# Fewer and larger transfers for the row-tile stacks and the maxima, values copied early, and the maxima split on GpSimd, in a float32 attention and FFN block

## What is computed

```python
x = x + attention(LN(x))      # 16 heads of 16: xw = x_h @ w_att_val[h]; softmax(xw @ x_h^T / 4) @ vx; out projection
x = x + ffn(LN(x))            # gate, up, down (704 wide); inputs, weights and h in blockwise FP4, silu(gate) * up
```

## Time and profile before

| | |
|---|---|
| median of 3 runs | 1744.99 us |
| the profiled execution, its own time | 1744.46 us |
| its span, first to last instruction | 1742.7 us |
| first block | 0 to about 55 us |
| stacks of batch 0, first max scores | 55 to 89 us |
| 16 batches of attention | 89 to about 1165 us |
| FFN | to 1742.7 us |
| PE busy over the span | 88% |
| DVE busy over the span | 77% |
| ACT, POOL busy over the span | 50%, 35% |

### The profile page before, as it was taken

One profiled execution on the slowest core, in us unless ns is written; L12 is line 12 of the kernel. 1 busy time (PEld: TensorE's weight loads), 2 busy tenths in 40 slices (PEclk: granted clock), 3 DMA queues, 4 the chain that ended last, 5 costly groups with the idle time before them and its releaser, 6 DMA issues. The chain is left out here.

```text
span 1742.7 us, 34245 instructions
## 1 busy us (share of the span) xinstructions
PE 1525.8 (88%) x8874; PEld 928.7 (53%) x8874; DVE 1343.5 (77%) x2731; ACT 866.4 (50%) x1778; POOL 605.2 (35%) x740
## 2 busy tenths in 40 slices
PE   3388888888898888888888989878999999999998
PEld 3144445455444454454454444445666666666666
DVE  7577676676686776766766857728999999999995
ACT  2056565565665655655656647653333333333332
POOL 2124324333333343243333332213334433333332
PEclk8589999998998998998999989998999999999999
DMA  4523343333343333333343333300000000000000
GB/s 153 147 75 106 105 111 98 101 100 106 93 111 92 107 100 99 110 98 105 100 102 98 110 89 97 113 2 3 19 15 15 15 15 15 15 15 15 15 18 18
DMA packets 82531, 127.34 MB, mean 73 GB/s; under 512 B 28864, under 2 KB 48448, under 8 KB 82368
## 3 DMA queue, kind: packets, MB, share of 16 engines
q1 hardware_dynamic: 74720, 119.55, 23.9%
q10 hardware_dynamic: 7776, 7.36, 1.4%
HBM read 81.67 MB, written 45.15 MB: 73 GB/s over the span
## 5 line engine op out<-in xcount | busy, mean ns | idle before, releaser
L1071 DVE TENSOR_REDUCE neg_max<-ring 128x1 f32<-128x512 f32 x1024 | 649.8, 679 | 212.8 <-PE ring L865 210.9
L1002 ACT ACTIVATE probs<-scores 128x512 f32<-128x512 f32 x1024 | 528.6, 604 | 273.5 <-PE scores L876 273.4
L865 PE MATMUL ring<-x_stack,q_stack 64*128 64x512 f32 x1024 | 247.3, 480 | 127.3 <-DVE o_rows L1123 49.4
L1408 PE MATMUL gu_bank<-splits,f_x_T 128*128 128x352 f32 x1024 | 317.4, 464 | 2.1 <-ACT f_x_T L1386 2.1
L892 PE MATMUL ring<-probs,v_quad 128*32 128x512 f32 x2048 | 279.6, 668 | 1.6 <-DVE o_rows L1123 0.8
L865 PEld LDWEIGHTS ring<-x_stack,q_stack 64*128 64x128 f32 x1024 | 103.3, 197 | 299.9 <-DVE neg_max L1071 152.6
L873 PE MATMUL scores<-q_stack,x_stack 64*128 64x512 f32 x1024 | 216.2, 417 | 36.4 <-DMA max_stack<-max_rows 35.9
L1408 PEld LDWEIGHTS gu_bank<-splits,f_x_T 128*128 128x128 f32 x1024 | 191.6, 192 | 99.3 <-issue 3.0
L723 POOL TENSOR_TENSOR pv_rows<-pv_more,pv_rows 128x512 f32<-128x512 f32 x64 | 82.2, 1284 | 422.3 <-ACT pv_more L1008 420.9
L876 PE MATMUL scores<-max_stack,max_ones 64*128 64x512 f32 x1024 | 211.4, 407 | 0.0
L1236 POOL TENSOR_TENSOR f_rstd<-f_mean_var,eps 128x1 f32<-128x1 f32 x64 | 44.7, 699 | 330.7 <-DVE f_mean_var L1346 330.7
(11 more groups left out here) (130 smaller groups left out, 2102.3 us busy)
## 6 DMA issues: line engine op xcount, KB each, us to landing
q_stack<-q_split SPq DMA_DIRECT2D x512, 64.0 KB, 2.4
x_stack<-x_split SPq DMA_DIRECT2D x256, 128.0 KB, 2.7
x_split<-splits SPq DMA_DIRECT2D x64, 256.0 KB, 2.2
q_split<-splits SPq DMA_DIRECT2D x64, 256.0 KB, 2.3
out_dram<-x_all SPq DMA_DIRECT2D x64, 128.0 KB, 1.7
x_all<-in_L_attn_x_dram ACTq DMA_DIRECT2D x14, 512.0 KB, 5.5
max_rows<-max_turned SPq DMA_DIRECT2D x256, 4.0 KB, 1.8
max_stack<-max_rows SPq DMA_DIRECT2D x128, 8.0 KB
```

Source lines behind the costliest of these rows:

```text
L865: pe.matmul(bank(tiles[m])[:, :], row_tile(q_stack[q], m)[:, p, s * P:(s + 1) * P], row_tile(x_stack[q], m)[:, p, :], start=True, stop=Tru ...
L1002: act.activation(probs[j][:, k, :], scores[k][:, :], ACT.Exp).then_inc(p_ready, 1)
L1071: dve.tensor_reduce(neg_max[g % 2][:, at:at + 1], tile[:, :], AX.X, ALU.max, negate=True).then_inc(m_used, 1)
L1408: m = pe.matmul(gu_bank[c][:, :], x_T[u][:, a, :], gate_up_T[:, a, c * CH:(c + 1) * CH], start=(a == 0), stop=(a == HALVES - 1))
```

## The change

The stacks are loaded with one transfer per row tile and tensor: 4 for a quad instead of 12. For this the stored keys are written four times, in the order of the row tile (xh, xl, xl, xh; the order of the pieces changes, and each key piece still meets the same query pieces: hh, lh, ll and hl in another order), and the query pieces are read twice by a source pattern with a leading dimension of two copies. The stored queries stay qh, ql; a q row tile is now qh, ql, qh, ql. The turned maxima go to DRAM with one transfer instead of four. GpSimd does the two splitting instructions of the maxima, DVE only the turn, one place later in the step. The copies of the values move to earlier steps of GpSimd's order. STORES counts six transfers of a half on one semaphore.

```diff
+STORES = (4 + 2) * 16
-    x_split = dram("x_split", [B, HALVES, 2, D, HH, T], F32)
-    q_split = dram("q_split", [B, HALVES, 2, D, HH, T], F32)
+    x_rows = dram("x_rows", [B, HALVES, 4, D, HH, T], F32)
+    q_rows = dram("q_rows", [B, HALVES, 2, D, HH, T], F32)
...
-                store(a, x_split, xh, xl, x_stored)
+                store(a, x_rows, (xh, xl, xl, xh))
...
-    POOL_STEP = {(0, 0): ("values",), (0, 1): ("halves", "x0"), (0, 3): ("q0",),
-                 (1, 0): ("values",), (1, 1): ("halves",),
-                 (2, 0): ("values",), (2, 1): ("halves", "x1"), (2, 2): ("deviation",), (2, 3): ("q1",),
-                 (3, 0): ("normal0", "values"), (3, 1): ("halves", "normal1"), (3, 2): ("normal2",),
+    POOL_STEP = {(0, 0): ("maxima", "values0"), (0, 1): ("halves", "x0", "values1"), (0, 3): ("q0", "values2"),
+                 (1, 0): ("maxima", "values3"), (1, 1): ("halves",),
+                 (2, 0): ("maxima",), (2, 1): ("halves", "x1"), (2, 2): ("deviation",), (2, 3): ("q1",),
+                 (3, 0): ("maxima", "normal0"), (3, 1): ("halves", "normal1"), (3, 2): ("normal2",),
                  (3, 3): ("normal3",)}
...
+            def split_maxima(i, g, start):
+                u, n = g % 2, QUAD * TT
+                pool.wait_ge(m_used, n * (i + 1))
+                if not start:
+                    pool.wait_ge(m_turned, i - 1)
+                pool.tensor_tensor(max_cols[u][:, 0:n].bitcast(F32R), neg_max[u][:, :],
+                                   one[:, :].broadcast_to([P, n]), ALU.mult).then_inc(m_split, 1)
+                pool.wait_ge(m_split, i + 1)
+                pool.tensor_tensor(max_cols[u][:, n:2 * n].bitcast(F32R), neg_max[u][:, :],
+                                   max_cols[u][:, 0:n], ALU.subtract).then_inc(m_low, 1)
...
                 for m in range(ROWS):
                     h = h0 + PAIRS * m
-                    for k in range(4):
-                        src = q_split[bass.ds(b, 1), a, k // 2, :, h:h + PAIRS, :]
-                        sp.dma_start(row_tile(q_stack[g], m)[D * k:D * k + D, :, :].bitcast(F32),
-                                     src.rearrange("o d h t -> (o d) h t")).then_inc(stack_loaded[g], 16)
-                    for k in range(2):
-                        src = x_split[bass.ds(b, 1), a, :, :, h:h + PAIRS, :]
-                        sp.dma_start(row_tile(x_stack[g], m)[2 * D * k:2 * D * k + 2 * D, :, :].bitcast(F32),
-                                     src.rearrange("o l d h t -> (o l d) h t")).then_inc(stack_loaded[g], 16)
+                    src = x_rows[bass.ds(b, 1), a, :, :, h:h + PAIRS, :]
+                    sp.dma_start(row_tile(x_stack[g], m).bitcast(F32),
+                                 src.rearrange("o k d h t -> (o k d) h t")).then_inc(stack_loaded[g], 16)
+                    src = q_rows[bass.ds(b, 1), a, :, :, h:h + PAIRS, :].rearrange("o k d h t -> (o k d) (h t)")
+                    sp.dma_start(row_tile(q_stack[g], m).bitcast(F32),
+                                 src.unsqueeze(0).broadcast_to([2, 2 * D, PAIRS * T])).then_inc(stack_loaded[g], 16)
...
                 sp.wait_ge(m_turned, i + 1)
-                for r in range(TT):
-                    sp.dma_start(max_rows[bass.ds(i, 1), :, r, :].rearrange("o c t -> (o c) t"),
-                                 max_turned[g % 2][32 * r:32 * r + 32, :]).then_inc(max_stored, 16)
-                sp.wait_ge(max_stored, 16 * TT * (i + 1))
+                sp.dma_start(max_rows[bass.ds(i, 1)].rearrange("o c r t -> (o r) c t"), max_turned[g % 2][:, :])\
+                  .then_inc(max_stored, 16)
+                sp.wait_ge(max_stored, 16 * (i + 1))
...
-            def max_part(part, i, g, start):
...
+            def turn_maxima(i, g, start):
+                dve.wait_ge(m_low, i + 1)
+                if not start:
+                    dve.wait_ge(max_stored, 16 * (i - 1))
+                dve.transpose(max_turned[g % 2][:, :], max_cols[g % 2][:, :]).then_inc(m_turned, 1)
...
-                        if j == 0 and s < 3 and turning:
-                            max_part(s, i + 1, (g + 1) % QUADS, first and g == 0)
+                        if j == 0 and s == 3 and turning:
+                            turn_maxima(i + 1, (g + 1) % QUADS, first and g == 0)
```

More of the change, by code:

```diff
@@ L112, in build @@
                 minus_half=minus_half, eps=eps, ident=ident, x_all=x_all, out_T=out_T, out_bias=out_bias,
-                x_split=x_split, q_split=q_split, gate_up_kept=gate_up_kept, down_kept=down_kept, sems=sems,
+                x_rows=x_rows, q_rows=q_rows, gate_up_kept=gate_up_kept, down_kept=down_kept, sems=sems,
             )
@@ L173, in first_block @@
                           "qh_done"))
-    x_stored, q_stored = ([sems[f"{n}_stored{a}"] for a in range(HALVES)] for n in "xq")
+    stored = [sems[f"stored{a}"] for a in range(HALVES)]
     x_first, gu_loaded, dn_loaded, vw_loaded, ow_loaded, qw_loaded, bias_loaded, kept = (
@@ L223, in load_x, with store @@
                              x[at:at + n].rearrange("b (s p) e -> p (b s) e", p=P)).then_inc(loaded, 16)
-            def store(a, dst, high, low, stored):
-                for k, t in enumerate((high, low)):
+            def store(a, dst, rows):
+                for k, t in enumerate(rows):
                     sp.dma_start(dst[0:1, a, k].rearrange("o d h t -> (o d h) t"), t[:, a, :].bitcast(F32))\
@@ L257, in _ @@
             for a in range(HALVES):
-                sp.wait_ge(x_stored[a], 32)
-                sp.wait_ge(q_stored[a], 32)
+                sp.wait_ge(stored[a], STORES)
             sp.wait_ge(kept, 16 * (len(GU_CHUNKS) + 2))
@@ L538, in attention_block @@
                           "qh_done"))
-    x_stored, q_stored = ([sems[f"{n}_stored{a}"] for a in range(HALVES)] for n in "xq")
+    stored = [sems[f"stored{a}"] for a in range(HALVES)]
     x_loaded, ffn_loaded = sem("x_loaded"), sem("ffn_loaded")
-    STACK = ROWS * 6 * 16
+    STACK = ROWS * 2 * 16
     pool_set, v_spread = sem("pool_set"), sem("v_spread")
@@ L754, in batch @@
                 first = isinstance(b, int) and b == 0
+                last = isinstance(b, int) and b == B - 1
                 for g in range(QUADS):
@@ L757, in batch @@
                         for task in POOL_STEP.get((g, j), ()):
-                            if task == "values":
-                                ready_values(b, g, first)
+                            if task == "maxima":
+                                if not (last and g == 3):
+                                    split_maxima(QUADS * b + g + 1, (g + 1) % QUADS, first and g == 0)
+                            elif task[:6] == "values":
+                                ready_values(b, int(task[6]), first)
                             elif task == "halves":
@@ L772, in _ @@
             pool.wait_ge(pool_set, set_up())
+            split_maxima(0, 0, True)
             batch(0)
@@ L783, in load_stacks, with store @@
                 a, h0 = g * QUAD // HH, g * QUAD % HH
-                sp.wait_ge(x_stored[a], 32 * (b + 1))
-                sp.wait_ge(q_stored[a], 32 * (b + 1))
+                sp.wait_ge(stored[a], STORES * (b + 1))
                 for m in range(ROWS):
                     h = h0 + PAIRS * m
-                    for k in range(4):
-                        src = q_split[bass.ds(b, 1), a, k // 2, :, h:h + PAIRS, :]
-                        sp.dma_start(row_tile(q_stack[g], m)[D * k:D * k + D, :, :].bitcast(F32),
-                                     src.rearrange("o d h t -> (o d) h t")).then_inc(stack_loaded[g], 16)
-                    for k in range(2):
-                        src = x_split[bass.ds(b, 1), a, :, :, h:h + PAIRS, :]
-                        sp.dma_start(row_tile(x_stack[g], m)[2 * D * k:2 * D * k + 2 * D, :, :].bitcast(F32),
-                                     src.rearrange("o l d h t -> (o l d) h t")).then_inc(stack_loaded[g], 16)
-            def store(c, a, dst, name, high, low, stored):
+                    src = x_rows[bass.ds(b, 1), a, :, :, h:h + PAIRS, :]
[4 more added lines that the diff above has]
+                                 src.unsqueeze(0).broadcast_to([2, 2 * D, PAIRS * T])).then_inc(stack_loaded[g], 16)
+            def store(c, a, dst, name, rows):
                 sp.wait_ge(x_low if name[0] == "x" else q_low, HALVES * (c - 1) + a + 1)
-                for k, t in enumerate((high, low)):
+                for k, t in enumerate(rows):
                     sp.dma_start(dst[bass.ds(c, 1), a, k].rearrange("o d h t -> (o d h) t"),
@@ L1171, in _ @@
                 if g == 0:
-                    for part in range(3):
-                        max_part(part, g, g, True)
+                    turn_maxima(g, g, True)
             batch(0)
```

35 lines of the change are left out of this document (10 added, 25 removed).

## The result

The changed kernel takes 2004.16 us (four runs, 1997.34 to 2015.10) against 1745.17 us for the kernel before, run beside it: ratio 1.149, 95% interval 1.143 to 1.155. It is 259 us slower. The forecast was 1927 us with a range of 1850 to 2120.

What follows compares the result with a forecast made beforehand. Bound taken: PE's stalls in the attention loop and the slow clock after them. Batch 78.8 us, 10.5 over 68.3, times 15 is 158; plus 24.5 before batch 0, sum 182 on 1744.46, giving 1927 us; range 1850 to 2120.

Steps and rivals of the forecast that it cites:

- The engines of a transfer: SyncE's transfers: q loads, whose pattern begins with 2, use 2 engines, 72 packets each per stack, 12.7 us.
- Cost of a packet: Stack loads on two engines: 0.176 us per 4 KB packet, ends 0.15 and 0.235; a stack lands after 14.9 us.
- 0.14 us: Packet time by the skill page's 27 GiB/s per engine; the sum would be some 80 us above today.
- The waits: PE waits for stacks or maxima at quad starts: 9.7 us at quad 2, none at 3, 5.7 at 0, 1.5 at 1.
- 3.8 + 17.6 = 21.4 against 15.7: Quad 0: q1 stored 3.8 us behind quad 2's end, maxima 17.6 later, quad 3 lasting 15.7; wait 5.7 us.
- The clock: PE's slow clock after a stall over 2 us: 2.0 us each behind the waits at quads 2 and 0.
- 57.9: Batch in us without the stalls: quads of 57.2 plus 0.7 for POOL being late in quad 1.
- Values early: Fourth values copy on POOL moves from (3, 0) to (1, 0), removing quad 3's stall: 5.8 us a batch gained.
- A: Quad 3's start: PE stalls 3.38 us behind DVE's v_dense and POOL's last values copy; 5.8 us a batch with slow clock.
- The maxima store: One SyncE issue for four saves 1.4 us per quad; its 128 B pieces stay as many.
- All 16 engines: Rival: all 16 engines serve the q loads, quad 2's stall also goes, batch 10.4 us less; 1586 us, chance 0.10.
- The rate of short transfers (2200 us): Rival: two engines at 0.235 us a packet, a stack 16.9 us, batch 96 us; 2200 us, chance 0.10.

Runs made afterwards that it cites:

- two q transfers: Changed kernel with each q_stack row tile loaded by two transfers of 32 rows instead of one beginning with 2; 1619.41 us, ratio 0.927 to the kernel before.
- the copies inside: Changed kernel, still one q load per row tile, but its source is 32 rows by 2 copies and q pieces are stored to match; 1646.88 us, ratio 0.943.
- The last two versions: Two q transfers with POOL's maxima first and even quads' maxima stored before stack loads, 1582.54 us; then also x tiles loaded before q is stored, 1571.17 us.
- the transfers alone: Changed kernel with the GpSimd part undone: new transfers, values and maxima as in the kernel before; 1980.50 us, ratio 1.135.

## Why the prediction was right

The direction, the cause and the range held; the time was 77 us too low. The packets of SyncE's queue on the page of the kernel before, for the first point:

```profile
q1 hardware_dynamic: 74720, 119.55, 23.9%
```

- **The engines of a transfer.** Read from the completions in the earlier trace rows, carried to the new pattern. The changed kernel's q1 has 70112 packets, 4608 fewer than the kernel before. The data and completion packets of the transfers that changed, with 2 engines for q and 4 for the maxima store, differ by just that: the key stores 9216 more, the x_stack loads 2048, the q_stack loads 7936 and the maxima stores 3840 fewer. With two q transfers it moved by the expected 3840, with x_stack on four engines by -1536 from there, and with the copies inside by 1792. The rule of the Trainium skill ("DMA: Bandwidth & Descriptors", How many engines (k)) agrees with all of them.
- **Cost of a packet.** Taken as 0.176 us. Measured 0.168 in 731 to 739 us (49 GB/s for two engines), 0.182 in 708 to 716 (45). The stack of quad 2 landed in 15.2 us in the batch shown and 16.0 in the mean, forecast 14.9; where the 1.1 us lie wasn't divided up. Before batch 0, 112.9 us against 113.9. The 0.14 us that the prediction also tried gives by its own sums 73 us over the kernel before, not some 80; neither of the two stretches shows such a packet.
- **The waits.** Forecast 1.5, 9.7, 0 and 5.7 us for quads 1, 2, 3 and 0, 16.9 in all; in the stretch shown 3.5, 6.8, about 0 and 9.5, 19.8 in all. So quads 2 and 0 come out nearly the other way round. Quad 2's is smaller since quad 1's stall and slow clock bring PE there 10.2 us after the stack's issue, where I had 8.0. The term that was short is quad 0's: "3.8 + 17.6 = 21.4 against 15.7". It had no x load in the queue. I had put 3 us for the x loads before batch 0 and forgot them in the loop, where one falls beside this very stack (18.0 us to land against 14.9). The run with the x load moved puts about 2 us on it; the rest is the slower stack itself. Quad 1's is larger since its stack took 17.0 us (701.00 to 718.03).
- **The clock.** I allowed 2.0 us behind two stalls. There are three, and by the key scores and the values' products behind them they cost 1.9, 2.9 and 2.0 us, 6.8 in place of 4.0. In the batch shown (702.30 to 785.50, 83.2 us) waits and clock are 5.7 us over the forecast, but the batch only 4.4: without them it is 56.6 us where I had 57.9. Over the six batches from 448.93 to 954.70, 84.3 us each, the waits average 21.8 us. So stalls and clock were forecast too small and the rest too large, and the two errors partly cancel: that the time came within 4% is in part luck.
- **Values early.** "I leave nothing of A" holds where it can show: 67 us alone, 81 with the split, against 87 less 10 expected. In the changed kernel it gains nothing, and with the split it costs 24 us. PE comes to quad 0's stack earlier and waits there (7.19 us against 2.85); that explains a gain of nothing, not the 24.
- **The maxima store,** costed at 1.4 us of SyncE and no more, is worth 27 us where the chain of quad 2 decides.
- **The rivals.** All 16 engines: 1586 us was forecast for that, and the run that grants it took 1619; its batch is 60.05 us where 57.9 was forecast. Half of the 2.1 us between them is the 1.1 us of wait for the maxima that it kept; the rest was not divided up. The last two versions came under 1586. The rate of short transfers (2200 us) did not appear: 32 packets in a row run at 0.17 to 0.18 us, not 0.235.

## What to carry to other kernels

Merging transfers saves issues, and here it is worth having: 1664 to 1619 us. But look at the first dimension of the merged transfer's patterns (these runs varied the one in DRAM), and keep a copy or a small outer count out of it when there are many bytes; count completion packets to see how many engines a transfer had. When a stall is removed ahead of a late transfer, the gain is only as good as that transfer's chain: shorten the chain first, and mind that a wait behind which the clock falls to half costs, here, some 2 us more (1.9 to 2.9 in the batch shown).

## What the runs showed of the hardware that I had not expected

When many transfers were outstanding on the two engines, the issue of the next one took long as well. Before batch 0 of the changed kernel SyncE's first six issues take 0.5 to 0.7 us each; the seventh takes 6.55, and of the later ones every x_stack load 4.85 to 5.87 and the maxima store 4.71 (timeline of its queue):

```profile
58.27 0.55 SPq L807 DMA_DIRECT2D q_stack<-q_rows  x1
58.86 6.55 SPq L804 DMA_DIRECT2D x_stack<-x_rows  x1
91.36 4.71 SPq L824 DMA_DIRECT2D max_rows<-max_turned  x1
```

In the run with two q transfers the same loads are issued without such holds; the longest stretch, two q issues together, takes 2.12 us. So transfers queued on two engines can hold up what stands behind them on the issuing engine, here x_stack loads, which have sixteen. And an x load of 512 KB issued by another engine, ACT, lands in 9.9 us instead of 5.5, beside either stack (9.9 as well in the run that moved it; 4.1 with the transfers alone, where it comes late in the stack's time). The likely reason is that a sixteenth of it lies on each of the two busy engines; the packets of one engine were not looked at.
